# Attention's query and key norms: the addition of epsilon moves from VectorE to GpSimd

## What is computed

```python
def rms_norm(x, w, eps=1e-6):
    var = jnp.mean(jnp.square(x), axis=-1, keepdims=True)
    return x * jax.lax.rsqrt(var + eps) * w
```

## Time and profile before

| | |
|---|---|
| median of 3 runs | 1548.42 us (1548.07 to 1552.4) |
| the profiled execution | 1551.07 us |
| its span, first to last instruction | 1549.8 us |
| busy: PE, DVE, ACT, POOL | 1489.0, 1136.7, 959.6, 691.8 us |
| mean granted TensorE clock | 0.992 |

### The profile page before, as it was taken

The page is one execution under the profiler, slowest core; times in us unless marked ns, Lnnn a source line. Parts: engine busy times, 40 slices in busy tenths (PEclk is TensorE's granted clock), DMA queues, the critical chain, the costliest instruction groups (busy, mean ns, idle before and its releaser), DMA issues. The chain is left out here.

```text
span 1549.8 us, 26210 instructions
## 1 busy us (share of the span) xinstructions
PE 1489.0 (96%) x8644; PEld 1164.4 (75%) x8644; DVE 1136.7 (73%) x2966; ACT 959.6 (62%) x2470; POOL 691.8 (45%) x832
## 2 busy tenths in 40 slices
PE   7999999999999999999999999999998799999988
PEld 5778888888888888888887665666656566666653
DVE  6787777777777767877788865555566888888774
ACT  5666666666666665666667764555546577666655
POOL 5564555465645554655566300000015455555544
PEclk9999999999999999999999999999999999999999
DMA  7011111111111111111145789788865301111000
GB/s 280 28 42 55 42 69 42 42 69 42 56 55 42 69 42 42 69 42 55 66 180 193 263 284 292 245 261 256 266 216 173 105 8 55 55 49 42 28 14 28
DMA packets 84327, 165.09 MB, mean 107 GB/s; under 512 B 39392, under 2 KB 39520, under 8 KB 82784
## 3 DMA queue, kind: packets, MB, share of 16 engines
q1 hardware_dynamic: 84192, 163.41, 30.8%
HBM read 113.05 MB, written 41.94 MB: 100 GB/s over the span
## 5 line engine op out<-in xcount | busy, mean ns | idle before, releaser
L617 ACT ACTIVATE Pt<-Pt,small 128x384 f32<-128x384 f32 (+1 forms) x256 | 172.8, 683 | 106.1 <-DVE small L877 106.0
L368 PE MATMUL bank<-wq,xT 128*128 128x512 f32 x768 | 207.6, 405 | 1.0 <-DVE wq L772 1.0
L421 PE MATMUL bank<-PT,vv 128*128 128x512 f32 x672 | 199.5, 405 | 5.5 <-DVE PT L862 4.7
L1135 POOL TENSOR_SCALAR Pt<-Pt,small 128x384 f32<-128x384 f32 (+1 forms) x256 | 164.0, 653 | 79.7 <-DVE small L885 79.6
L877 DVE CUSTOM_DVE_ANT_0 Pt<-quad,mask,small 128x384 f32<-128x384 f32 (+1 forms) x256 | 171.9, 680 | 30.5 <-PE quad L398 29.2
L1356 PE MATMUL bank<-wq,ot 128*128 128x512 f32 x768 | 182.0, 394 | 1.0 <-DMA ot<-ot_scratch 1.0
L862 DVE TENSOR_TENSOR PT<-quad,PT 128x512 fp32r<-128x512 f32 x224 | 154.1, 688 | 38.4 <-ACT PT L609 37.9
L1356 PEld LDWEIGHTS bank<-wq,ot 128*128 128x128 f32 x768 | 143.9, 188 | 33.0 <-DMA ot<-ot_scratch 1.4
L368 PEld LDWEIGHTS bank<-wq,xT 128*128 128x128 f32 x768 | 137.2, 189 | 26.5 <-DVE wq L772 2.3
L1123 POOL TENSOR_TENSOR t<-t 128x512 f32<-128x512 f32 x64 | 83.6, 1306 | 145.2 <-DVE t L843 145.2
L421 PEld LDWEIGHTS bank<-PT,vv 128*128 128x128 f32 x672 | 116.4, 189 | 29.8 <-DVE PT L862 11.0
(11 more groups left out here) (286 smaller groups left out, 3500.0 us busy)
## 6 DMA issues: line engine op xcount, KB each, us to landing
ot_scratch<-OT SPq DMA_DIRECT2D x64, 512.0 KB, 2.6
ot<-ot_scratch SPq DMA_DIRECT2D x64, 512.0 KB, 5.8
wkv_f<-in_w SPq DMA_DIRECT2D x12, 512.0 KB, 6.2
wkc_f<-in_w SPq DMA_DIRECT2D x12, 512.0 KB, 6.4
wkv_f<-in_wg SPq DMA_DIRECT2D x11, 512.0 KB, 7.1
wkv_f<-in_wd SPq DMA_DIRECT2D x11, 512.0 KB, 7.1
wkv_f<-in_wu SPq DMA_DIRECT2D x10, 512.0 KB, 7.4
stg<-in_ctxT SPq DMA_DIRECT2D x16, 256.0 KB, 4.1
```

The source lines that it names most:

```text
L368: ins = pe.matmul(bQ[:], xT[p][:, k, qt * 128:qt * 128 + 128], wq[j][:, g, k, :], start=(part == 0 and k == 0), stop=(part == 2 and k == 3))
L421: ins = pe.matmul(bO[:], vv[x][:, bg % 2, kt, :], PT[y][:, k % 2, :], start=(kt == 0 and n == 0), stop=(kt == tiles_in(i) - 1 and n == 2))
L617: act.activation(p, p, ACT.Exp, bias=nm[:, i % 2, h:h + 1], scale=-1.0, accum_out=sm[:, i % 2, h:h + 1]).then_inc(f["s_exp"], 1)
L1135: pool.tensor_scalar(p, p, ri[:, i % 2, h:h + 1], 1.0, ALU.mult, ALU.mult).then_inc(f["p_n"], 1)
```

## The change

For queries and keys the addition of 128e-6 is taken from VectorE's program (`dve_q_ve`, `dve_k_ss` and all their calls) and put on GpSimd, directly ahead of the power and with a wait between the two. GpSimd now waits for the sums of squares themselves (`q_sq`, `k_sq`). The semaphores `q_ve` and `k_ve` go. To keep ScalarE from overwriting sums that GpSimd still needs, `act_k_sq` waits for the power of the unit before, and `act_q_sq` for that of the block before; `pool_k_rs` waits until VectorE has used the factors of the unit before.

```diff
     def act_k_sq(u, queries=None):
...
         act.wait_ge(f["kv_mm"], u + 1)
-        if u in (1, 3):
-            act.wait_ge(f["k_ve"], u)
+        after(act, f["k_rs"], u)
         if u:
             act.wait_ge(f["q_sq"], queries or u)
...
     def act_q_sq(i, keys=None):
...
         act.wait_ge(f["k_sq"], keys or i + 1)
+        after(act, f["q_rs"], i)
...
-    def dve_k_ss(u):
-        if u >= NU:
-            return
-        dve.wait_ge(f["k_sq"], u + 1)
-        dve.tensor_scalar(kve[:, 0:2], kss[:, 0:2], 128e-6, None, ALU.add).then_inc(f["k_ve"], 1)
...
-    def dve_q_ve(i):
-        if i >= NBLK:
-            return
-        dve.wait_ge(f["q_sq"], i + 1)
-        dve.tensor_scalar(qve, qss, 128e-6, None, ALU.add).then_inc(f["q_ve"], 1)
...
     def pool_k_rs(u):
         if u >= NU:
             return
-        pool.wait_ge(f["k_ve"], u + 1)
+        pool.wait_ge(f["k_sq"], u + 1)
+        after(pool, f["k_n"], u)
+        g_.did(pool.tensor_scalar(kve[:, 0:2], kss[:, 0:2], 128e-6, None, ALU.add))
+        g_.settle()
         pool.tensor_tensor(krs[:, 0:2], kve[:, 0:2], half[:, 0:2], ALU.pow).then_inc(f["k_rs"], 1)
...
     def pool_q_rs(i):
         if i >= NBLK:
             return
-        pool.wait_ge(f["q_ve"], i + 1)
+        pool.wait_ge(f["q_sq"], i + 1)
+        g_.did(pool.tensor_scalar(qve, qss, 128e-6, None, ALU.add))
+        g_.settle()
         pool.tensor_tensor(cq[:, i % 2, :], qve, half[:, 0:4], ALU.pow).then_inc(f["q_rs"], 1)
```

More of the change, by code:

```diff
@@ L934, in dve_even @@
             dve_w(2 * i + 5)
-        dve_q_ve(i + 1)
         dve_p_lo(i - 1, 1)
@@ L939, in dve_even @@
         dve_ri(i, 0)
-        dve_k_ss(i + 2)
         dve_last(i, 0)
@@ L984, in dve_odd @@
         dve_p_lo(i - 1, 1 if i > 1 else 2)
-        if i > 1:
-            dve_k_ss(i + 2)
         dve_last(i, 0)
@@ L1041, in dve_program @@
                                      rope[:, cs:cs + 2, :], ALU.mult, ALU.mult).then_inc(f["tables"], 1)
-        dve_k_ss(0)
         dve_w(2)
@@ L1051, in dve_program @@
         dve_w(4)
-        dve_q_ve(0)
-        dve_k_ss(1)
         dve_k_n(1)
@@ L1067, in dve_program @@
         dve_ri(0, 1)
-        dve_k_ss(2)
-        dve_q_ve(1)
         dve_w(6)
         dve_k_n(2)
-        dve_k_ss(3)
         dve_w(7)
@@ L2584 @@
 c_hi c_lo ln_var ln_rs ln_x xt_mm xt_hi xt_lo
-kv_mm k_sq k_ve k_rs k_n k_rope kt_mm kt_hi kt_lo v_hi v_lo
-q_mm q_sq q_rope q_add q_ve q_rs qt_mm qt_hi qt_lo
+kv_mm k_sq k_rs k_n k_rope kt_mm kt_hi kt_lo v_hi v_lo
+q_mm q_sq q_rope q_add q_rs qt_mm qt_hi qt_lo
 s_mm s_ev s_exp s_ri p_n pt_mm pt_hi pt_lo pv_mm o_hi o_lo ot0
```

## The result

| | before | after |
|---|---|---|
| median of 13 runs each, us | 1550.07 (1547.26 to 1552.4) | 1552.68 (1549.67 to 1555.93) |
| ratio after / before | | 1.0024, 95% interval 1.0016 to 1.0033 |
| the profiled execution: time, span, us | 1551.07, 1549.8 | 1552.77, 1551.5 |

A forecast was written before the change was run, and what follows sets the result against it. The prediction took TensorE's full queue as the bound; 2.9 + 0.6 + 0.2 - 0.7 = +3.0 us gave 1554.1 against the profiled 1551.07, or 1551.4 on the scale of the runs' median, range 1545 to 1557.

The forecast's parts named there:

- What goes: 0 in quiet blocks: Attention blocks where TensorE is full: removing 128 VectorE additions, about 22 us of work, saves 0.
- 0.32 us an addition: Cost of each GpSimd addition: 0.24 us fixed plus 0.08 for the wait; range 0.08 to 0.55.
- Preparing blocks, +2.9: Seven blocks with i % 8 == 5: two additions lengthen GpSimd's gapless run, +4.5 us, less 1.6; bounds -0.5 and +6.1.
- The late load, -1.6: Two preparing blocks: the DMA of x is issued up to 1 us earlier, so the statistics' wait vanishes, -1.6 us.
- The start, +0.6: First units: VectorE's weight split may come before q_add and delay the key's factor, +0.4, others +0.2; bounds -0.3 and +1.5.
- blocks 2 and 4, +0.2: There a weight split stands beside the key's power, +0.2 us; bounds -0.4 and +0.8.
- Block 60, -0.7: Without the key's addition VectorE's sums over the feed-forward weight start 0.7 us earlier: -0.7 us.
- The slower one: Rival: GpSimd's addition is dear in the preparing blocks' gapless run; at 0.55 us, +6.2; decides from 0.44; chance 0.22.
- No effect: Rival: PE is full and the rest cancels, additions near 0.1 us, sum within 1 us of 0; chance 0.21.
- Faster: Rival: VectorE's relief wins through PE's waits, block 60 and the start, -4.9 us, 1543.5; chance 0.07.

The follow-up runs named there:

- no_add: The changed kernel with the epsilon additions of the first attention left out on both engines; ordinary preparing block 15.55 us, against 16.42 in the changed kernel.
- twice: The changed kernel with each addition made as two halves of 64e-6 on GpSimd; ordinary preparing block 17.09 us, against 16.42 in the changed kernel.
- tt_add: The changed kernel with each addition a tensor_tensor reading epsilon from a constant tile, not an immediate; ordinary preparing block 16.10 us, against 16.42 in the changed kernel.
- q_only: The kernel before with the query's addition alone moved to GpSimd; ordinary preparing block 16.01 us, against 15.50 before.
- late_add: The kernel before with VectorE's query addition put behind o_lo and p_lo in preparing blocks; all seven take 15.68 us, against 15.50 for ordinary ones before.
- before_again: The kernel before, unchanged, profiled a second time; span 1545.7 us against 1549.8, ordinary preparing block 15.50 us.
- before_swap: The kernel before with GpSimd's key power ahead of the first two softmax divisions in preparing blocks; 1546.86 us, ratio 0.9982 to before.
- after_swap: The changed kernel with GpSimd's key power ahead of the first two softmax divisions in preparing blocks; 1546.1 us, ratio 0.9975 to before.
- mixed_swap: The kernel after_swap with the key's addition back on VectorE in the seven preparing blocks only; 1542.41 us, ratio 0.9957 to before.
- k_only: The kernel before with the key's addition alone moved to GpSimd; ordinary preparing block 15.96 us against 15.50 before, block 60 12.27 against 13.14.

## Why the prediction was right, and where its terms were not

The forecast was +3.0 us, within 0.3%, and +3.7 was measured. The place and the mechanism were right, one price was too low, and the start was priced too high, so part of the agreement is luck. The terms, in its order:

- **What goes: 0 in quiet blocks.** Right: 25.53 us before and after, and each quiet block within 0.04 us. no_add shows more, that the relief of VectorE is worth nothing in ordinary preparing blocks either. The removed additions are 29.3 us by their own durations, since nine of the 128 were held; the forecast said about 22. VectorE's busy time fell by only 18.6, because it counts once what neighbouring records overlap.
- **0.32 us an addition.** The step that failed; it measured 0.46, over the 0.4 and over the 0.44 at which the forecast called itself wrong and the rival decisive. The instruction's 0.24 and the wait's 0.08 were right, in the block and in twice. Missing was the 0.13 in front: I priced the instruction and the gap behind it, and took for granted that it would follow its forerunner as closely as the others do. tt_add ties this to the addition with an immediate number. L1135, which the forecast called the same kind of instruction, reads its factor from a tile and starts on time, and a fit of its durations could not have shown a late start.
- **Preparing blocks, +2.9.** Measured: 4.7 in the five ordinary ones, +0.21 and -0.19 in 37 and 45, together +4.7. With 0.46 for 0.32 the forecast's own working gives 14 x 0.46 - 1.6 = 4.8. The place was right: the wait of VectorE grew from 0.57 to 1.95, PE's from nothing to 1.39, and PE's other product is on time. The key's power comes 0.9 us later against the context subtractions, not 0.6 (421.45 - 414.45 = 7.00, against 6.09).
- **The late load, -1.6.** Right in mechanism, as q_only and late_add show. Against an ordinary block, 37 and 45 came out (0.93 - 0.21) + (0.93 + 0.19) = 1.84 us better.
- **The start, +0.6, and blocks 2 and 4, +0.2.** The collision came as worked out for the order in which the split is first: +0.41 at the key's factor for "+0.4". From block 0 to block 5, though, the profile of after is 0.2 us shorter than that of before (71.70 against 71.91). One pair cannot settle this. Four kernels have the start of before (before, before_again, late_add, before_swap) and take 71.33 to 71.91 us for these blocks, in the mean 71.6; three have that of after (after, after_swap, mixed_swap) and take 71.70 to 72.22, in the mean 71.9. So the term lies near +0.3, with as much scatter, and below the +0.8 of the sum. Blocks 2 and 4 add nothing to it: each is within 0.04 us of before. Why the 0.41 was gone by block 1 in the profile of after I did not find out; stretches of half clock at 39.8 us before and 37.9 us after lie just there. The start of block 0 itself I leave out: it moves from 26.71 to 27.98 us between profiles whatever the kernel, and to 30.06 in before_swap.
- **Block 60, -0.7.** -0.88, and it goes with the key's addition alone (k_only, not q_only).

The sum of the measured terms is 4.7 - 0.2 - 0.9 = +3.6 us by the one pair of profiles, or +4.1 with +0.3 for the start, beside +3.7 (2.5 to 5.1) by the ratio. So the forecast came closer than its terms: the preparing blocks were underrated by 1.8 us (2.0 for the additions, less 0.2 for the load), and the start and block 60 overrated by 0.7 to 1.2 together.

**The rivals.** The slower one named the right place, and its threshold, 0.44 us an addition, was passed by the 0.46 measured. What kept the whole under 0.3% was the start, which came out lower than in its sum, and block 60. "No effect" needed additions near 0.1. "Faster" needed a VectorE that binds and a GpSimd run that does not grow: no_add, with VectorE relieved and nothing added, gains 2.7 us in blocks 37, 45 and 60 and nothing in the five ordinary ones, and in the changed kernel the run grew by 0.92.

## What to carry to other kernels

A step moved off an engine with idle time gains nothing by itself; what it costs is read at the places where the receiving engine's queue runs without a gap and somebody waits at its end. Here that was one stretch in seven blocks of 64, and inside it a moved instruction counts with its gaps on both sides. Once such a wait is known, try the order within the receiving queue before the placement of the work: putting the awaited power ahead of two divisions was worth 1.14 us a block, more than both additions cost. The gain depends on what waits: in the kernel before the same move gave 0.25.

## What the runs showed of the hardware

- A GpSimd addition of two or four columns with an immediate takes 0.24 us and starts 0.08 to 0.09 us after the instruction ahead of it ends. With a second tensor in place of the immediate it takes 0.20 and starts 0.04 us before that end.
- A VectorE addition of four columns takes about 0.17 us, and 1.05 or 1.23 when it begins under a GpSimd subtraction or addition of 512 columns, with which it then ends. Under a GpSimd power it keeps its 0.16. It works the other way as well: GpSimd's addition took 1.02 for 0.24 beside the weight split, and q_add 2.26 for 1.29.
- The number of half-clock stretches is no property of the kernel. Two profiles of one program, before and before_again, differ by a stretch at 9.1 us and one at 944 us, and their spans by 4.1 us. From 9.2 to 12.4 us, and again from 944.4 to 947.6, the granted clock is 0.50 in the one and 1.00 in the other.
